# First stage's output projection with the weights stationary: the sum is kept transposed, copied once per batch and turned back

## The chip, the cores and the metric

The kernel runs on one core of one Trainium2 chip. The metric is the device time of one execution in microseconds (us), from the first to the last work of that core. A core has five engines with their own instruction streams: PE (TensorE, matrix products; its weight loads are shown apart as PEld), DVE (VectorE), ACT (ScalarE), POOL (GpSimd) and SP (SyncE, which here only issues DMAs). They wait for one another through semaphores.

## The reference, cut to what matters

A block with 16 batches of 512 tokens and 128 channels. First attention with 16 heads of 64 over a band of 33 keys, then a feed-forward part with attention and a mixture of eight experts. The change touches the last product of the first part and the gate behind it:

```python
h = _layernorm(x, axis=-1) * (1 + ca) + sa
# attention: xn = rms_norm(h); q, k, v; rope; banded softmax; out = attn @ v
out = out.transpose(0, 2, 1, 3).reshape(B, T, H * D)     # (16, 512, 1024)
return out @ w_out.T                                     # (16, 512, 128)
x = x + ga * _L0_attn_ref(h, ...)                        # ga: one gate per batch and channel
```

## The kernel before, in words

The first stage works on items. An item is one batch and one pair of heads (`G = 8` pairs per batch, `NI = 128` items, item i is batch i // 8). Every engine runs the same loop over slots `s`, and each step of an item has a fixed lag behind the slot that starts it: rope of item s, scores of item s-2 (`LS`), softmax of item s-3 (`LE`), transposes of the probabilities of item s-4 (`LT`), the product with the values of item s-5 (`LV`) and the output projection of item s-6 (`LO`). So the order of the work on each engine is written out by hand; only semaphores decide when it starts.

In one slot PE issues, in this order: two rope groups (`matmul` lines 305 to 307, each three products with 512 columns moving, into a PJ bank), the output projection (line 317), 16 small score products (line 331), 16 small products with the values (line 347), in some slots `to_columns` (line 262), then `values` (lines 281 to 283, one group of three into a PJ bank) and eight transposes of probabilities (line 366).

The output projection multiplies the attention output `ot`, which lies with the item's 128 head channels on the partitions and the 512 tokens along the row. Four products per item take 128 tokens each as the stationary operand and the item's `wo` as the moving one; they add up over the batch's eight items in the PSUM bank `ACC` as four blocks of tokens x channels. After the eighth item DVE multiplies `ACC` by the gate in `mod` into `x1` (line 485), POOL adds `xt` (line 569), and SP stores `x1` and loads the input of a later batch (lines 233 and 180). A product with f32 operands appears in the trace as two records.

**The PJ ring.** Two PSUM banks (`PJ`) are used in turn by everything that has to be read back at once: rope groups, `values`, the columns of the next batch's normalized input (`xn`, in slots with s % 8 == 6) and a gate row (`mod`, in slots with s % 8 == 3). The list `plan` holds the uses in order. Before PE writes a use, `bank_of` waits until the use two places earlier in `plan` has been read:

```python
n = pj_use[w]
if n >= 2:
    v = plan[n - 2]
```

What it waits for depends on the kind of that use: for a rope group DVE's second product (line 458), for `values` ACT's copy into `vn` (line 655), and for `xn` the semaphore `s_xl`. The last comes from a chain: `to_columns(b)` on PE, then ACT copies the bank into `xh` (`x_high`, line 596), then DVE writes the rest, bank minus `xh`, into `xl` (`x_low`, line 400). `xh` and `xl` of a batch are what rope and `values` of its items read, from the slot after next on.

ACT works through a slot in the order: two copies into `pT` (line 624), eight exponentials (line 633), the copy into `ot` (line 642), `x_high` in slots with s % 8 == 6, and the copy into `vn` (line 655). DVE's order is: four rope products (lines 457 and 458), eight masked row maxima (line 469), a reciprocal (line 478), line 485 in slots with s % 8 == 5 from s = 13 on, `x_low` in slots with s % 8 == 6. SP issues per slot four DMAs of `sw` (line 207) and two or three of `vw` (lines 217 to 220).

Of the kernel before, what the change touches and what calls it, by code (L numbers as in the profile page):

```python
# [14 lines left out]
P = 128  # L15
NB, T, C = 16, 512, 128
NH, G = 16, 8
NI = NB * G
# [11 lines left out]
def program(nc, a, out, debug=None):  # L30
# [6 lines left out]
    with top:  # L37
        def sbt(ctx, name, shape, dt=F32):
            return ctx.enter_context(nc.sbuf_tensor(name, shape, dt))

        def sem(name):
            return top.enter_context(nc.semaphore(name))
# [3 lines left out]
        ident = sbt(top, "ident", [P, P])  # L46
# [14 lines left out]
        p1 = ExitStack()  # L61
        mod = sbt(p1, "mod", [P, NB, 3 * C])
# [4 lines left out]
        wo = sbt(p1, "wo", [P, G, C])  # L67
# [4 lines left out]
        xn = sbt(p1, "xn", [P, 4, C])  # L72
# [31 lines left out]
        sq = sbt(p1, "sq", [P, C])  # L104
        ot = [sbt(p1, f"ot{n}", [P, T]) for n in range(2)]
        x1 = [sbt(p1, f"x1{n}", [P, 4, C]) for n in range(2)]

        s_x = [sem(f"a_x{n}") for n in range(4)]
        s_ct = sem("a_ct")
# [29 lines left out]
        s_pj = sem("a_pj")  # L139
# [13 lines left out]
        s_ot = sem("a_ot")  # L153
        s_op = sem("a_op")
        s_y = sem("a_y")
        s_x1 = sem("a_xo")
        s_x1d = [sem("a_x1d0"), sem("a_x1d1")]

# [2 lines left out]
        SLOTS = NI + LO + 1  # L161

        plan = [("xn", 0)]
        for s in range(NI):
            plan += [("rope", s, 0), ("rope", s, 1)]
            if s % G == 6 and s // G + 1 < NB:
                plan.append(("xn", s // G + 1))
            if s % G == 3 and s // G + 2 <= NB:
                plan.append(("mod", s // G + 2))
            plan.append(("v", s))  # L170
        pj_use = {w: n for n, w in enumerate(plan)}

        def vd_count(n):
# [2 lines left out]
        with nc.Block() as blk:  # L176
            @blk.sync
            def _(sp):
                def x_in(b):
                    sp.dma_start(xt[b % 4][:, :, :], x_d[:, 4 * b:4 * b + 4, :]).then_inc(s_x[b % 4], 16)  # L180

                x_in(0)
                sp.dma_start(ct[:, :], a["ct"]).then_inc(s_ct, 16)
                for n in range(2):
                    c = slice(384 * n, 384 * n + 384)
                    sp.dma_start(wmod[:, c], a["wmod"][:, c]).then_inc(s_wm[n], 16)
                    if n == 0:
                        sp.dma_start(ident[:, :], a["ident"]).then_inc(s_id, 16)
                for n in range(3):
                    c = slice(1024 * n, 1024 * n + 1024)  # L190
                    sp.dma_start(wf3[:, c], a["wqkv"][:, c]).then_inc(s_wf[n], 16)
                sp.dma_start(cos[:, :], a["cos"]).then_inc(s_cs, 16)
                sp.dma_start(sin[:, :], a["sin"]).then_inc(s_cs, 16)
                sp.dma_start(mf[:, :], a["masks"]).then_inc(s_mf, 16)
                sp.dma_start(wo[:, :, :], a["wo"]).then_inc(s_wo, 16)
                sp.dma_start(b1t[:, :], a["b1"]).then_inc(s_b1, 16)
                for b in range(1, 4):
                    x_in(b)
                sp.wait_ge(s_z, 2)
                for s in range(SLOTS):  # L200
                    if s < NI:
                        sp.wait_ge(s_rope, 2 * s + 2)
                        if s >= 2:
                            sp.wait_ge(s_add, s - 1)
                        for k in range(4):
                            d, m = slice(32 * k, 32 * k + 32), slice(32 * (k ^ 1), 32 * (k ^ 1) + 32)
                            sp.dma_start(sw[s % 2][d, :, :], mm[s % 2][m, 1, :, :]).then_inc(s_sw[s % 2], 16)
                        half, j = divmod(s, 4)
                        v = vw[half % 2]
                        if half >= 2:  # L210
                            sp.wait_ge(s_pv, 4 * (half - 2) + 4)
                        else:
                            sp.wait_ge(s_zi, 1)
                            sp.wait_ge(s_wlo, 3)
                            sp.wait_ge(s_mk, 3)
                        sp.wait_ge(s_ve, s + 1)
                        sp.dma_start(v[32:96, 2 * j, :], vn[j][0:64, :]).then_inc(s_vd[j], 16)
                        sp.dma_start(v[0:96, 2 * j + 1, :], vn[j][32:128, :]).then_inc(s_vd[j], 16)
                        if j < 3:
                            sp.dma_start(v[0:32, 2 * j + 2, :], vn[j][96:128, :]).then_inc(s_vd[j], 16)  # L220
                    if s == NI - 8:
                        for dst, src in ((bc[:, :, :].rearrange("p a b -> p (a b)"), "bc"), (wfa, "fw"), (con, "con"),
                                         (rows, "rows"), (trf, "tri")):
                            sp.dma_start(dst[:, :], a[src]).then_inc(s_l2, 16)
                        sp.dma_start(bkf[:, :], a["blk"][:, 0:P]).then_inc(s_l2, 16)
                        for e in range(2):
                            sp.dma_start(w1s[e][:, :], a["W1"][:, e * DF:(e + 1) * DF]).then_inc(s_ws[e], 16)
                    if s < NE:
                        sp.dma_start(xs_d[NE * STR + s * P:NE * STR + (s + 1) * P, :], zrow[:, :]).then_inc(s_pre, 16)
                    if s >= LO and (s - LO) % G == G - 1:  # L230
                        b = (s - LO) // G
                        sp.wait_ge(s_x1, b + 1)
                        sp.dma_start(x1_d.rearrange("(j p) b c -> b p j c", p=P)[b], x1[b % 2][:, :, :])\
                          .then_inc(s_x1d[b % 2], 16)
                        if b + 4 < NB:
                            x_in(b + 4)
                sp.wait_ge(s_x1d[0], 16 * (NB // 2))
                sp.wait_ge(s_x1d[1], 16 * (NB // 2))
                sp.wait_ge(s_pre, 16 * NE)
                sp.wait_ge(s_b1, 16)  # L240

            @blk.tensor
            def _(pe):
                def bank_of(w):
# [3 lines that stand above are left out]
                        if v[0] == "rope":  # L248
                            pe.wait_ge(s_rope, 2 * v[1] + v[2] + 1)
                        elif v[0] == "v":  # L250
                            pe.wait_ge(s_ve, v[1] + 1)
                        elif v[0] == "mod":
                            pe.wait_ge(s_mev, v[1] + 1)
                        else:
                            pe.wait_ge(s_xl, v[1] + 1)
                    return PJ[n % 2]
# [38 lines left out]
                for s in range(SLOTS):  # L295
# [13 lines left out]
                    if 0 <= i < NI:  # L309
                        b, g = divmod(i, G)  # L310
                        pe.wait_ge(s_ot, i + 1)
                        if i == 0:
                            pe.wait_ge(s_wo, 16)
                        if g == 0 and b:
                            pe.wait_ge(s_y, b)
                        for j in range(4):
                            ins = pe.matmul(ACC[:, j * P:(j + 1) * P], ot[i % 2][:, j * P:(j + 1) * P], wo[:, g, :],  # L317
                                            start=(g == 0 and j == 0), stop=(g == G - 1), skip_group_check=True)
                        ins.then_inc(s_op, 1)
                    i = s - LS  # L320
                    if 0 <= i < NI:
                        if i:
# [28 lines left out]
                    if s < NI:  # L351
                        if s % G == 6 and s // G + 1 < NB:
                            to_columns(s // G + 1)
                        if s % G == 3 and s // G + 2 <= NB:
                            spread(s // G + 2, bank_of(("mod", s // G + 2)))
                        values(s)
                    i = s - LT
                    if 0 <= i < NI:
# [11 lines left out]
            def _(dve):  # L370
# [76 lines left out]
                for s in range(SLOTS):  # L447
# [32 lines left out]
                    if 0 <= i < NI and i % G == G - 1:  # L480
                        b = i // G
                        dve.wait_ge(s_op, i + 1)
                        if b >= 2:
                            dve.wait_ge(s_x1d[b % 2], 16 * (b // 2))
                        dve.tensor_tensor(x1[b % 2][:, :, :], ACC[:, :].rearrange("p (j c) -> p j c", j=4),
                                          mod[:, b:b + 1, 2 * C:].to_broadcast([P, 4, C]), ALU.mult).then_inc(s_y, 1)
                    b, r = s // G + 1, s % G
                    if b < NB:
# [8 lines left out]
            def _(pool):  # L497
# [45 lines left out]
                for s in range(SLOTS):  # L543
# [14 lines left out]
                    if b < NB:  # L558
# [3 lines left out]
                            next(sh)  # L562
                        if r == 4:
                            scale(b)
                    i = s - LO
                    if 0 <= i < NI and i % G == G - 1:
                        b = i // G
                        pool.wait_ge(s_y, b + 1)
# [943 lines left out]
```

## Time and profile before

| | us |
|---|---|
| median of three runs | 1257.46 (1255.93 to 1259.2) |
| the profiled execution | 1253.87 |
| its span, first to last instruction | 1252.1 |
| first stage, from PE's first slot to its last projection | 21.8 to 824.3 |
| PE busy over the span | 1127.8 (90%) |
| ACT, POOL, DVE busy | 931.4, 873.5, 871.3 |
| mean granted clock of TensorE, share of full | 0.952 |

A row of a timeline gives the start, how long it took, the engine, the line, the operation, what it writes and reads, and how many records were merged; in brackets the idle time of the engine before it and what ended that. Records of PE overlap: each lasts until its result is written, while the next may have started; so the time that a group takes from PE is the distance between the starts of two groups, not the sum of the records' lengths.

### The profile page before, as it was taken

Reading aid. Unit: us, or ns where it says so; the run is one execution under the profiler, and the core shown is the slowest. Engines: PE = TensorE matmul, PEld = TensorE weight load, DVE = VectorE, ACT = ScalarE, POOL = GpSimd, SP = SyncE. Lnnn points to the kernel's source line nnn. Section 1 sums busy time; section 2 is a strip of 40 time slices with the busy share of each in tenths; the row PEclk is TensorE's granted clock in tenths of the full one; section 3 lists DMA queues with packets and bytes.
Section 4 is the critical chain, followed back from the end, with each engine's and each line's share of the span. In section 5 each row is a group of like instructions: output and inputs, shape, how many; then the busy total and the mean of one; then the engine's idle time right before and its main releaser. Section 6 shows DMA issues by size and latency. Waiting matters only on the chain. (4 is left out here: it accounts for less than half of the span.)

```text
span 1252.1 us, 50490 instructions
## 1 busy us (share of the span) xinstructions
PE 1127.8 (90%) x18097; PEld 957.1 (76%) x18097; DVE 871.3 (70%) x4013; ACT 931.4 (74%) x3429; POOL 873.5 (70%) x705
## 2 busy tenths in 40 slices
PE   4899999999999999999999999948889883599991
PEld 2688888888888888888888888836678773588881
DVE  6777777777786777877777866636678864177663
ACT  3789888889889898898898898837767652366660
POOL 3787776777777777767777776645466777178885
PEclk9999999999999999999999999979989985699996
DMA  5766666666666666666666667524143224575110
GB/s 175 200 175 164 160 158 161 150 170 158 153 170 157 158 164 147 166 160 151 168 165 148 161 157 189 139 87 153 50 133 95 73 79 154 159 199 153 56 34 24
DMA packets 108262, 177.55 MB, mean 142 GB/s; under 512 B 19294, under 2 KB 61537, under 8 KB 107888
## 3 DMA queue, kind: packets, MB, share of 16 engines
q1 hardware_dynamic: 100176, 155.14, 48.3%
q0 software_dynamic: 6400, 16.82, 3.8%
q8 instruction: 148, 2.42, 0.8%
q10 hardware_dynamic: 1440, 2.36, 0.7%
q14 instruction: 98, 0.80, 0.2%
HBM read 31.86 MB, written 24.68 MB: 45 GB/s over the span
## 5 line engine op out<-in xcount | busy, mean ns | idle before, releaser
L549 POOL TENSOR_TENSOR qk<-mm,sw 128x1024 f32<-128x1024 f32 x128 | 303.9, 2374 | 120.5 <-DMA sw<-mm 120.5
L633 ACT ACTIVATE pr<-sm,mn 128x96 f32<-128x96 f32 x1024 | 368.5, 370 | 0.2 <-DVE mn L469 0.2
L457 DVE TENSOR_TENSOR mm<-bank,cos 128x512 f32<-128x512 f32 x256 | 175.3, 685 | 175.6 <-PE bank L307 165.5
L555 POOL TENSOR_TENSOR pr<-pr,ri 128x768 f32<-128x768 f32 x128 | 188.2, 1470 | 77.2 <-DVE ri L478 75.2
L633 ACT ACTIVATION_READ_ACCUMULATOR pr<-sm,mn 128x1 f32 x1024 | 201.9, 197 | 0.0
L469 DVE CUSTOM_DVE_ANT_0 sm<-bank,msk 128x96 f32<-128x96 f32 x1024 | 192.0, 252 | 5.3 <-PE bank L331 5.3
L458 DVE TENSOR_TENSOR mm<-bank,sin 128x512 f32<-128x512 f32 x256 | 174.0, 680 | 0.0
L347 PE MATMUL bank<-pT,vw 96*64 96x64 f32 x4096 | 147.5, 225 | 0.0
L317 PEld LDWEIGHTS bank<-wo,ot 128*128 128x128 f32 x1024 | 133.4, 191 | 14.2 <-ACT ot L642 3.2
L347 PEld LDWEIGHTS bank<-pT,vw 96*64 96x64 f32 x4096 | 129.8, 138 | 15.2
L624 ACT ACTIVATE pT<-bank 96x512 f32<-96x512 f32 x256 | 137.3, 588 | 0.0
L317 PE MATMUL bank<-wo,ot 128*128 128x128 f32 x1024 | 135.1, 275 | 2.3 <-ACT ot L642 2.3
L366 PE MATMUL bank<-ident,pr 128*96 128x128 f32 x1024 | 132.7, 273 | 0.0
L366 PEld LDWEIGHTS bank<-ident,pr 128*96 128x96 f32 x1024 | 115.7, 126 | 18.7
L1225 ACT ACTIVATE fv<-bank,b1t 128x128 f32<-128x128 f32 x288 | 82.2, 368 | 54.8 <-PE bank L1088 53.6
L642 ACT ACTIVATE ot<-bank 128x512 f32<-128x512 f32 x128 | 76.2, 595 | 62.0 <-PE bank L347 62.0
L305 PE MATMUL bank<-xh,wh 128*128 128x512 f32 x256 | 113.8, 444 | 4.6 <-DVE xl L400 1.4
L331 PE MATMUL bank<-qk 64*64 64x96 f32 x4096 | 114.1, 249 | 2.9 <-POOL qk L549 2.9
L655 ACT ACTIVATE vn<-bank 128x512 f32<-128x512 f32 x128 | 76.2, 595 | 42.7 <-PE bank L283 42.7
L331 PEld LDWEIGHTS bank<-qk 64*64 64x64 f32 x4096 | 89.9, 133 | 19.7 <-issue 2.9
L306 PE MATMUL bank<-xl,wh 128*128 128x512 f32 x256 | 101.9, 398 | 0.0
L307 PE MATMUL bank<-xh,wl 128*128 128x512 f32 x256 | 101.6, 397 | 0.0
(195 smaller groups left out, 2333.0 us busy)
## 6 DMA issues: line engine op xcount, KB each, us to landing
sw<-mm SPq DMA_DIRECT2D x512, 128.0 KB, 2.3
vw<-vn SPq DMA_DIRECT2D x128, 192.0 KB, 2.5
vw<-vn SPq DMA_DIRECT2D x128, 128.0 KB, 2.3
rr<-sorted_scratch SPq DMA_DIRECT2D x72, 192.5 KB, 3.0
vw<-vn SPq DMA_DIRECT2D x96, 64.0 KB, 2.2
xt<-in_x SPq DMA_DIRECT2D x16, 256.0 KB, 4.3
x_scratch<-x SPq DMA_DIRECT2D x16, 256.0 KB, 2.7
rr<-x_scratch SPq DMA_DIRECT2D x16, 256.0 KB, 3.0
```

The source lines that it names most:

```text
L305: pe.matmul(dst[:, :], wh[:, o:o + P], xh[b % 2][:, :], start=True, stop=False)
L317: ins = pe.matmul(ACC[:, j * P:(j + 1) * P], ot[i % 2][:, j * P:(j + 1) * P], wo[:, g, :], start=(g == 0 and j == 0), stop=(g == G - 1), s ...
L331: ins = pe.matmul(SC[h][64 * e:64 * e + 64, p * WK:(p + 1) * WK], t[r, 0, 32 + 64 * w:96 + 64 * w], t[r, 1, 64 * w:64 * w + WK], start=Tru ...
L347: ins = pe.matmul(OB[64 * h:64 * h + 64, 64 * w:64 * w + 64], vw[half % 2][:, w, c:c + 64], pT[i % 2][:, h, 64 * w:64 * w + 64], start=Tru ...
L366: ins = pe.transpose(TR[h][0:WK, p * P:(p + 1) * P], pr[i % 2][:, h, p, :], ident[:, :])
L457: dve.tensor_tensor(mm[s % 2][:, 0, j, :], PJ[u % 2][:, :], cos[:, :], ALU.mult)
L458: dve.tensor_tensor(mm[s % 2][:, 1, j, :], PJ[u % 2][:, :], sin[:, :], ALU.mult)\
L469: ins = dve.tensor_tensor_reduce(ms_[i % 2][:, h, p, :], SC[h][:, p * WK:(p + 1) * WK], msk[:, min(p, 1), :], 1.0, 3.0e38, ALU.add, ALU.mi ...
L549: pool.tensor_tensor(qk[i % 2][:, :, 32:], mm[i % 2][:, 0, :, :], sw[i % 2][:, :, :], ALU.add)\
L555: pool.tensor_tensor(t, t, ri[i % 2][:, :].unsqueeze(2).to_broadcast([P, 8, WK]), ALU.mult)\
L624: act.activation(pT[i % 2][:, h, :], TR[h][0:WK, :], ACT.Copy).then_inc(s_te, 1)
L633: ins = act.activation(pr[i % 2][:, h, p, :], ms_[i % 2][:, h, p, :], ACT.Exp, scale=-1.0, bias=mn[i % 2][:, h, p:p + 1], accum_out=sums[i ...
```

## The change

The output projection swaps its operands. `wo` of the item is stationary and all 512 tokens of `ot` move, in one product per item; `ACC` then holds the sum transposed, channels x tokens. After the batch's eighth item DVE copies it into a new tile `yt`. One slot later PE turns `yt` back by four transposes into a PJ bank, and DVE multiplies that bank by the gate. So `plan` has a new use, `yt`, before `values` in every slot with s = 14, 22, ..., 134, and POOL's addition and SP's store and load move one slot later. PE's wait before the first projection of a batch is for the copy (`s_yt`) and no longer for the gate product (`s_y`).

```diff
-        for s in range(NI):
-            plan += [("rope", s, 0), ("rope", s, 1)]
...
+        for s in range(SLOTS):
+            if s < NI:
+                plan += [("rope", s, 0), ("rope", s, 1)]
+                if s % G == 6 and s // G + 1 < NB:
+                    plan.append(("xn", s // G + 1))
+                if s % G == 3 and s // G + 2 <= NB:
+                    plan.append(("mod", s // G + 2))
+            if s > LO and (s - LO - 1) % G == G - 1:
+                plan.append(("yt", (s - LO - 1) // G))
+            if s < NI:
+                plan.append(("v", s))
...
+                        elif v[0] == "yt":
+                            pe.wait_ge(s_y, v[1] + 1)
...
-                            pe.wait_ge(s_y, b)
-                        for j in range(4):
-                            ins = pe.matmul(ACC[:, j * P:(j + 1) * P], ot[i % 2][:, j * P:(j + 1) * P], wo[:, g, :],
-                                            start=(g == 0 and j == 0), stop=(g == G - 1), skip_group_check=True)
-                        ins.then_inc(s_op, 1)
+                            pe.wait_ge(s_yt, b)
+                        pe.matmul(ACC[:, :], wo[:, g, :], ot[i % 2][:, :], start=(g == 0), stop=(g == G - 1))\
+                            .then_inc(s_op, 1)
...
+                    i = s - LO - 1
+                    if 0 <= i < NI and i % G == G - 1:
+                        b = i // G
+                        dst = bank_of(("yt", b))
+                        pe.wait_ge(s_yt, b + 1)
+                        for j in range(4):
+                            ins = pe.transpose(dst[:, j * P:(j + 1) * P], yt[:, j * P:(j + 1) * P], ident[:, :])
+                        ins.then_inc(s_pj, 1)
+                    if s < NI:
                         values(s)
...
                         dve.wait_ge(s_op, i + 1)
+                        if b:
+                            dve.wait_ge(s_pj, pj_use[("yt", b - 1)] + 1)
+                        dve.tensor_copy(yt[:, :], ACC[:, :]).then_inc(s_yt, 1)
+                    i = s - LO - 1
+                    if 0 <= i < NI and i % G == G - 1:
+                        b = i // G
+                        u = pj_use[("yt", b)]
+                        dve.wait_ge(s_pj, u + 1)
                         if b >= 2:
                             dve.wait_ge(s_x1d[b % 2], 16 * (b // 2))
-                        dve.tensor_tensor(x1[b % 2][:, :, :], ACC[:, :].rearrange("p (j c) -> p j c", j=4),
+                        dve.tensor_tensor(x1[b % 2][:, :, :], PJ[u % 2][:, :].rearrange("p (j c) -> p j c", j=4),
                                           mod[:, b:b + 1, 2 * C:].to_broadcast([P, 4, C]), ALU.mult).then_inc(s_y, 1)
```

PE's rows in slot 14 before, from the last product with the values to the next slot's first rope group (`a_xl` is the semaphore `s_xl`, `a_rope` is `s_rope`):

```order
245 L262 MATMUL bank<-ident,xn 128x128 [waits a_xn,a_rope]
246 L262 MATMUL bank<-ident,xn 128x128 x3
247 L281 MATMUL bank<-wh,xh 128x512 [waits a_rope]
248 L282 MATMUL bank<-wl,xh 128x512
249 L283 MATMUL bank<-wh,xl 128x512
250 L366 MATMUL bank<-ident,pr 96x128 [waits a_te,a_nm]
251 L366 MATMUL bank<-ident,pr 96x128 x3
252 L366 MATMUL bank<-ident,pr 96x128 [waits a_te]
253 L366 MATMUL bank<-ident,pr 96x128 x3
254 L305 MATMUL bank<-xh,wh 128x512 [waits a_xl]
```

The same place of the changed kernel, whose lines 270, 289 and 313 are lines 262, 281 and 305 of before, and whose line 381 is line 366:

```order
236 L270 MATMUL bank<-ident,xn 128x128 [waits a_xn,a_rope]
237 L270 MATMUL bank<-ident,xn 128x128 x3
238 L368 MATMUL bank<-ident,yt 128x128 [waits a_yt,a_rope]
239 L368 MATMUL bank<-ident,yt 128x128 x3
240 L289 MATMUL bank<-wh,xh 128x512 [waits a_xl]
241 L290 MATMUL bank<-wl,xh 128x512
242 L291 MATMUL bank<-wh,xl 128x512
243 L381 MATMUL bank<-ident,pr 96x128 [waits a_te,a_nm]
244 L381 MATMUL bank<-ident,pr 96x128 x3
245 L381 MATMUL bank<-ident,pr 96x128 [waits a_te]
246 L381 MATMUL bank<-ident,pr 96x128 x3
247 L313 MATMUL bank<-xh,wh 128x512 [waits a_y]
```

The four transposes of `yt` stand between `xn` and `values`; the wait for `s_xl` has moved from the next slot's rope group up to `values`, and the rope group waits for `s_y`.

DVE's rows in the changed kernel at the end of the maxima of the same slot (`a_pj` counts PE's finished uses of the ring; `x` is `x1`); before, the reciprocal was followed by `xl` at once:

```order
323 L493 RECIPROCAL ri<-sums 128x8 [waits a_nm,a_exp]
324 L508 TENSOR_TENSOR x<-bank,mod 128x512 [waits a_pj]
325 L415 TENSOR_TENSOR xl<-bank,xh 128x512 [waits a_xh]
326 L472 TENSOR_TENSOR mm<-bank,cos 128x512 [waits a_sw1,a_add,a_pj]
```

The gate product has come from the slot before to a place ahead of `x_low`.

## Rows read from the trace of the kernel before

**Rows 1.** The page: busy us and shares; the projection's group, mean ns behind the bar

```profile
PE 1127.8 (90%) x18097; PEld 957.1 (76%) x18097; DVE 871.3 (70%) x4013; ACT 931.4 (74%) x3429; POOL 873.5 (70%) x705
...
L317 PE MATMUL bank<-wo,ot 128*128 128x128 f32 x1024 | 135.1, 275 | 2.3 <-ACT ot L642 2.3
```

**Rows 2.** Windows: busy time of each engine in one batch (eight slots)

```profile
361.52:410.81 49.29, 49.16 (x722) 42.20 (x719) 37.08 (x184) 43.38 (x176) 36.40 (x24) 1.00 0.64 160
```

**Rows 3.** Waits, 65 to 755 us: total, times, longest

```profile
PEld bank L305 <- DVE xl L400: 5.4, 14, 0.4
```

**Rows 4.** Timeline of PE, parts of two undisturbed slots

```profile
780.67 0.39 PE L306 MATMUL bank<-xl,wh 128*128 128x512 f32 x1
780.89 0.39 PE L307 MATMUL bank<-xh,wl 128*128 128x512 f32 x1
...
781.83 1.05 PE L317 MATMUL bank<-wo,ot 128*128 128x128 f32 x8
782.81 0.89 PE L331 MATMUL bank<-qk 64*64 64x96 f32 x32
...
787.79 1.05 PE L317 MATMUL bank<-wo,ot 128*128 128x128 f32 x8
```

**Rows 5.** Timeline of PEld in the second stage, f32 with 512 moving

```profile
855.74 0.30 PEld L1000 LDWEIGHTS bank<-hT,wfa 128*128 128x128 f32 x2
856.27 0.19 PEld L1000 LDWEIGHTS bank<-hT,wfa 128*128 128x128 f32 x1 [0.24 <-issue]
856.70 0.19 PEld L1000 LDWEIGHTS bank<-hT,wfa 128*128 128x128 f32 x1 [0.24 <-issue]
```

**Rows 6.** Timeline of PE in a slot with xn

```profile
402.47 0.66 PE L262 MATMUL bank<-ident,xn 128*128 128x128 f32 x4
402.88 0.48 PE L281 MATMUL bank<-wh,xh 128*128 128x512 f32 x1
...
404.84 0.50 PE L305 MATMUL bank<-xh,wh 128*128 128x512 f32 x1
```

**Rows 7.** Timeline of ACT in the same slot and the next

```profile
403.00 0.59 ACT L642 ACTIVATE ot<-bank 128x512 f32<-128x512 f32 x1
403.47 0.59 ACT L596 ACTIVATE xh<-bank 128x512 fp32r<-128x512 f32 x1
...
409.33 0.60 ACT L642 ACTIVATE ot<-bank 128x512 f32<-128x512 f32 x1 [0.96 <-PE bank L347]
```

**Rows 8.** Timeline of DVE, the slot before and the slot with xn

```profile
397.11 0.64 DVE L485 TENSOR_TENSOR x<-bank,mod 128x512 f32<-128x512 f32 x1
...
404.09 0.69 DVE L400 TENSOR_TENSOR xl<-bank,xh 128x512 fp32r<-128x512 f32 x1 [0.76 <-ACT xh L596]
```

**Rows 9.** Timeline of the first stage's end, PE and DVE

```profile
823.13 1.16 PE L317 MATMUL bank<-wo,ot 128*128 128x128 f32 x8 [0.69 <-ACT ot L642]
...
824.33 0.69 DVE L485 TENSOR_TENSOR x<-bank,mod 128x512 f32<-128x512 f32 x1 [7.46 <-PE bank L317]
...
829.20 0.45 PE L967 MATMUL bank<-ident,bc 128*128 128x128 f32 x1 [4.91 <-PEq L176]
```

**Rows 10.** Timeline of SP's DMA issues in the slot with xn and the next

```profile
405.98 0.81 SPq L217 DMA_DIRECT2D vw<-vn  x1
...
407.47 0.60 SPq L220 DMA_DIRECT2D vw<-vn  x1
408.35 2.42 SPq L207 DMA_DIRECT2D sw<-mm  x4
```

**Rows 11.** Timeline of POOL, behind them

```profile
408.11 2.38 POOL L549 TENSOR_TENSOR qk<-mm,sw 128x1024 f32<-128x1024 f32 x1 [3.23 <-DMA sw<-mm]
```

**Rows 12.** Windows: columns as in rows 2, with the granted clock as a share

```profile
30.00:35.00 5.00, 2.52 (x39) 1.75 (x38) 2.28 (x6) 0.06 (x1) 3.62 (x2) 1.00 0.86 224
35.50:38.90 3.40, 3.26 (x11) 1.97 (x14) 1.96 (x18) 2.92 (x14) 2.67 (x2) 0.51 0.80 225
...
815.00:824.00 9.00, 7.26 (x107) 6.50 (x104) 0.20 (x1) 5.34 (x17) 1.47 (x1) 1.00 0.02 4
```

More of the change, by code:

```diff
@@ L106, in program @@
         x1 = [sbt(p1, f"x1{n}", [P, 4, C]) for n in range(2)]
+        yt = sbt(p1, "yt", [P, T])
         s_x = [sem(f"a_x{n}") for n in range(4)]
@@ L155, in program @@
         s_y = sem("a_y")
+        s_yt = sem("a_yt")
         s_x1 = sem("a_xo")
@@ L163, in program @@
         plan = [("xn", 0)]
-        for s in range(NI):
-            plan += [("rope", s, 0), ("rope", s, 1)]
[L166 to L170, printed above, removed]
+        for s in range(SLOTS):
[9 more added lines that the diff above has]
+                plan.append(("v", s))
         pj_use = {w: n for n, w in enumerate(plan)}
@@ L229, in _ @@
                         sp.dma_start(xs_d[NE * STR + s * P:NE * STR + (s + 1) * P, :], zrow[:, :]).then_inc(s_pre, 16)
-                    if s >= LO and (s - LO) % G == G - 1:
-                        b = (s - LO) // G
+                    if s > LO and (s - LO - 1) % G == G - 1:
+                        b = (s - LO - 1) // G
                         sp.wait_ge(s_x1, b + 1)
@@ L564, in _ @@
                             scale(b)
-                    i = s - LO
+                    i = s - LO - 1
                     if 0 <= i < NI and i % G == G - 1:
```

## The prediction

> **What bounds the kernel now.** I began with the page's busy shares [rows 1]: PE leads with 90% of the whole span, but that mixes two stages. The windows over one batch of the first stage [rows 2] separate them: in 49.29 us PE is busy for 49.16, at the full clock, while ACT has 43.38 and DVE 37.08. The waits of the stage say where the little rest is: PE waits in only one place that counts, 14 times before line 305, 5.4 us in all [rows 3]. So in the first stage every microsecond that PE gains or loses is the kernel's. A slot takes PE 5.96 us from projection to projection [rows 4], and 128 of them make up the stage.
>
> The one wait of PE deserves the close look, because the change passes through it. It stands in the slots with `xn`. There [rows 6] PE turns `xn` at 402.47, goes on with `values` at 402.88 and the transposes of probabilities, and arrives at the next rope group before its bank is free; that group starts at 404.84. What it waited for is a chain on two other engines. ACT comes out of its exponentials at 403.0, copies `ot`, and then writes `xh` from 403.47 to 404.06 [rows 7]. DVE has waited 0.76 us for that and writes `xl` from 404.09 to 404.78 [rows 8]. Today PE covers most of this chain with `values` and line 366.
>
> **The projection itself.** It removes 8 records per item and adds 2. Today the 8 take 1.05 us to the last one's end; with 0.27 us for the last record itself (the mean in [rows 1]) they follow one another every (1.05 - 0.27) / 7 = 0.111 us, so 8 use 0.89 us. From the first to the start of line 331 it is 0.98 us [rows 4], so that 0.09 us belongs to the change of tile shape ahead of line 331; I leave it. The nearest rows for the new form are line 1000's, the same f32 type and 128x128 weights with 512 columns moving. Their weight loads, one per record, follow every 0.43 us at full clock [rows 5]. Two make 0.86 us. So four times the columns cost four times the time, and an item gains 0.03 us: 128 x 0.03 = 4 us. The weight loads that disappear (six per item) were hidden behind the products and return nothing. Bounds: at best the long second record also hides the 0.09, and an item gains 0.12 us, 15 us in all; at worst the first record pays what line 1000's first pays (0.53 against 0.43, from the load at 855.74 to that at 856.27, after another tile shape), and an item loses 0.07, 9 us in all. I take 0.03, because the product ahead of the projection (line 307) has the full tile shape and is long enough to cover a load of 0.19.
>
> Against this stands a rule. The Trainium skill, "TensorE: Matmul & The Clock Gate", section "Back-to-back issue gap", gives for sustained streams of load and product about 81 ns each with 128 columns and 131 ns with 512; by it, four products of 128 would become one of 512 at 131 / 324 = 0.40 of their time, 0.98 would become 0.40 us, and 128 items would gain some 75 us. No row here shows such a gap for f32: [rows 5] have 0.43 us per record of 512, four times the 0.111 of [rows 4].
>
> **The four transposes.** 4 records of f32 per batch at the same 0.11 us: 0.44 us of PE. In slot 126, where there is no `xn`, that is all: the gate product is then covered by `values` and line 366.
>
> **The ring.** This is the large term. `yt` takes a place in `plan` between `xn` and `values`. `values` used to wait for the slot's second rope group, long read; two places back it now finds `xn`, and that means `s_xl`: PE stands before `values`, without the 1.6 us of work that used to cover the chain. Also, DVE has the gate product ahead of `x_low`. Worked out for the slot of [rows 6]:
> - line 262 ends at 402.47 + 0.66 = 403.13; the transposes of `yt` follow and end 0.44 later, 403.57.
> - the gate product, 0.64 us [rows 8], runs from 403.61 to 404.25. `xh` is ready at 404.06 [rows 7], so it is no longer what is late.
> - `x_low` can start a little before that end (DVE's products follow about 0.6 apart), at 404.20, and ends 0.69 later, 404.89.
> - PE begins `values` 0.06 after it, as line 305 does today (404.78 to 404.84): 404.95 where it was 402.88.
> - from `values` to the rope group is 404.84 - 402.88 - 0.38 of waiting = 1.58 us, and 0.03 more for a start from idle: 406.56 against 404.84.
>
> The batch loses 1.7 us on PE, the 0.44 of the transposes included. It happens where `xn` and `yt` meet: slots 14, 22, ..., 118, 14 times: 23.8 us. Bounds: 1.6 if DVE's order cost nothing and only ACT's copy counted; 1.9 if DVE starts the gate product later than I put it.
>
> What is late next: `vn` is copied when `values` is done, about 405.9 to 406.5 instead of 403.95, so ACT starts the next slot about 2.1 us late while PE is 1.7 late. ACT has 0.96 us of waiting before its next `ot` [rows 7], which covers 0.4. SP waits for `vn` before its three issues; they begin at 406.5 rather than 405.98 and take 2.1 [rows 10], and the store and load that the change moves into this slot add some 1.2: 409.9. The next `sw` is due at 408.35 + 1.7 = 410.05. That just fits, and behind it POOL idles 3.23 us for `sw` [rows 11]. POOL's addition, which moves in there, fits too. I cost all three at nothing.
>
> **The end of the stage.** After the last projection comes the chain PE, DVE, POOL, store, and then the second stage's first PE row at 829.20 [rows 9], covered by nothing. It gets a copy (0.69), the transposes from idle (0.66 + 0.1) and two hand-overs (0.09): 1.5 us. The copies of the other batches take the place of a gate product of the same size on DVE [rows 8], which had been finished at 397.75, long before it was wanted; nothing.
>
> **The sum.** 14 x 1.7 + 0.44 + 1.5 - 4 = +21.7 us on the profiled execution's 1253.87, which gives 1275.6. The median of the runs shown is 3.6 us above that execution, so the median should be 1257.46 + 21.7 = 1279. Differences under 0.3%, 3.8 us, are about what a measurement of this kernel cannot tell from none.
>
> **Rivals.**
> - *The stall costs more* (11 in 100). Either the clock falls in it, or the SP queue, which has only 0.15 us to spare, makes the next slot late. For the clock: after a stretch in which PE was busy for 2.52 of 5 us it ran at 0.51, which is the 1.2 GHz level, for 3.4 us [rows 12]; in the stage's last slots, 7.26 of 9 busy, it stayed at 2.4 GHz. The new slot is idle for about 1.5 us at one time and dense on both sides, nearer to the second. If it fell for one such stretch per batch, PE would lose half of 3.26 us each time: 14 x 1.6 = 23 us more, 1302; in half of the batches 1290.
> - *The wait is covered anyway* (4 in 100): `x_low` would have to end by 403.3, when PE is through with `yt`. The rows give 404.78 even without the gate product in front. Then the sum is 15 x 0.44 + 1.5 - 4 = +4, 1261, and within 0.3% if the 0.09 of line 331 is hidden in part.
> - *The projection gets much cheaper* (5 in 100; this one ends faster). If f32 with 512 moving ran at the pace of lines 306 to 307, 0.23 us from start to start [rows 4], an item would take 0.46 + 0.09 = 0.55 instead of 0.98: 55 us gained against 26 lost, 1228. It decides from 0.2 us per item on (26 / 128). For it: one load instead of four per pass, and the rule above. Against it: line 1000's records do not run at that pace in this same kernel [rows 5].
>
> **The numbers.** My case has 80 in 100. Its own range comes from the bounds: item gain 15 gives 1268, item loss 9 gives 1292, and 1.6 to 1.9 per batch moves it by -1 to +3. The range 1268 to 1292 leaves out the two rivals below it, 9 in 100, and most of the one above. Faster by over 0.3%: 0.05. Within 0.3%: 0.04. Slower: 0.91.
>
> **What the profile after would show.** If I am right: two records per item some 0.43 apart and about 0.95 us from the projection to the scores; slots without a new use at 5.92 to 5.93 instead of 5.96; in every eighth slot PE idle for some 1.5 us before `values`, released by `x_low`, and no wait left before the rope group; that slot 1.7 longer; the first stage's end 1.5 later than its last projection explains; the clock at full. I am wrong if the pair of records is under 0.4 us (then faster), or if the wait stands but the next slot is also longer (then the first rival).

## The result and the profile after

The changed kernel takes 1277.58 us (median, 1275.91 to 1282.43) where the kernel before took 1257.35 in the same session: 1.0173 times the time, with a 95% interval from 1.0141 to 1.0205. It is 20.2 us slower; the forecast was 21.7 slower, 1279. Ratios compare fast executions only: one of the kernel with the copies swapped and the loads spread, 1422.61 us at a granted clock of 0.73, counts in its median but not in its ratio.

The profiled execution is the slowest of the four, 1282.43 us. So I read it in two parts, cut where PE starts the second stage, at 829.20 before [rows 9] and at 851.17 now. The first stage has become 22.0 us longer. The windows over the second stage, which the change does not touch, first of the kernel before and then of the changed one (length, busy time and records of PE, PEld, DVE, ACT and POOL, granted clock, busy share of the DMA engines, GB/s):

```profile
829.20:1252.10 422.90, 329.46 (x6603) 279.39 (x6603) 270.21 (x1078) 231.70 (x639) 281.32 (x326) 0.86 0.35 107
```

```profile
851.20:1280.60 429.40, 336.90 (x6603) 286.03 (x6603) 271.09 (x1078) 232.19 (x639) 282.67 (x326) 0.83 0.35 105
```

It has the same 6603 records of PE and took 6.5 us more in this execution, at a mean clock of 0.83 instead of 0.86. Over all the kernels profiled here it takes 421 to 429 us, with no relation to what was edited. The first stage is the place to compare.

The page of the changed kernel, busy shares and the projection's group:

```profile
PE 1138.8 (89%) x17393; PEld 886.3 (69%) x17393; DVE 882.8 (69%) x4029; ACT 933.9 (73%) x3429; POOL 874.6 (68%) x705
...
L324 PE MATMUL bank<-ot,wo 128*128 128x512 f32 x256 | 131.0, 593 | 2.4 <-ACT ot L665 2.4
```

1024 records have become 256, each about twice as long. PE is busy 11 us longer than before [rows 1] although it has fewer instructions; 7.4 of the 11 lie in the second stage (336.90 against 329.46). One batch (columns as in [rows 2]):

```profile
370.04:420.73 50.69, 49.31 (x677) 37.28 (x675) 37.52 (x184) 43.55 (x175) 36.73 (x24) 1.00 0.62 154
```

A batch takes 50.69 us instead of 49.29, and PE is no longer busy in all of it: 1.38 us are idle. The waits from 65 to 770 us say where:

```profile
ACT vn L678 <- PE bank L291: 51.3, 98, 1.8
...
PEld bank L289 <- DVE xl L415: 22.6, 14, 1.6
PE bank L289 <- DVE xl L415: 19.3, 14, 1.4
...
DVE x L508 <- PE bank L368: 3.1, 14, 0.2
```

The wait of [rows 3] before the rope group is gone. In its place PE stands 14 times before `values` (line 289), 19.3 us in all, until DVE has written `xl`. And ACT, which waited up to 0.4 us for `values`, now waits up to 1.8. An undisturbed slot on PE, beside [rows 4]:

```profile
802.11 1.02 PE L324 MATMUL bank<-ot,wo 128*128 128x512 f32 x2
803.06 0.89 PE L337 MATMUL bank<-qk 64*64 64x96 f32 x32
...
808.03 1.02 PE L324 MATMUL bank<-ot,wo 128*128 128x512 f32 x2
```

The projection takes 0.95 us to the start of the scores instead of 0.98, and the slot 5.92 instead of 5.96. The slot with `xn` and `yt`, PE, beside [rows 6]:

```profile
410.85 0.66 PE L270 MATMUL bank<-ident,xn 128*128 128x128 f32 x4
411.35 0.60 PE L368 MATMUL bank<-ident,yt 128*128 128x128 f32 x4
413.33 0.50 PE L289 MATMUL bank<-wh,xh 128*128 128x512 f32 x1 [1.38 <-DVE xl L415]
...
414.92 0.47 PE L313 MATMUL bank<-xh,wh 128*128 128x512 f32 x1
```

The same stretch on DVE, beside [rows 8]:

```profile
411.55 0.20 DVE L493 RECIPROCAL ri<-sums 128x8 f32<-128x8 f32 x1
411.98 0.69 DVE L508 TENSOR_TENSOR x<-bank,mod 128x512 f32<-128x512 f32 x1 [0.23 <-PE bank L368]
412.59 0.68 DVE L415 TENSOR_TENSOR xl<-bank,xh 128x512 fp32r<-128x512 f32 x1
```

And on ACT, beside [rows 7]:

```profile
411.89 0.59 ACT L619 ACTIVATE xh<-bank 128x512 fp32r<-128x512 f32 x1
414.32 0.60 ACT L678 ACTIVATE vn<-bank 128x512 f32<-128x512 f32 x1 [1.84 <-PE bank L291]
...
419.36 0.60 ACT L665 ACTIVATE ot<-bank 128x512 f32<-128x512 f32 x1 [0.60 <-PE bank L353]
```

From line 270 to `values` it is 2.48 us where it was 0.41; from there to the rope group 1.59. The transposes of `yt` end at 411.95, DVE takes the bank at 411.98, starts `xl` 0.61 later, and PE goes on 0.06 after its end. What SP does behind it:

```profile
414.99 0.50 SPq L223 DMA_DIRECT2D vw<-vn  x1
...
417.45 0.53 SPq L186 DMA_DIRECT2D xt<-in_x  x1
418.40 3.29 SPq L213 DMA_DIRECT2D sw<-mm  x4
```

SP is through at 417.98 and is wanted at 418.40. The end of the stage, beside [rows 9]:

```profile
843.63 1.12 PE L324 MATMUL bank<-ot,wo 128*128 128x512 f32 x2 [0.69 <-ACT ot L665]
844.79 0.69 DVE L500 COPY yt<-bank 128x512 f32<-128x512 f32 x1 [7.40 <-PE bank L324]
...
845.63 0.63 PE L368 MATMUL bank<-ident,yt 128*128 128x128 f32 x4 [0.88 <-DVE yt L500]
846.29 0.69 DVE L508 TENSOR_TENSOR x<-bank,mod 128x512 f32<-128x512 f32 x1 [0.81 <-PE bank L368]
...
851.17 0.45 PE L990 MATMUL bank<-ident,bc 128*128 128x128 f32 x1 [4.91 <-PEq L182]
```

From the start of the last projection to the second stage it is 7.54 us, against 6.07 before: 1.5 more.

### The profile page after: what moved, and what is told of

Read it like the earlier page. It is cut to its first block and busy times, and to the rows that moved or that the text cites. A ratio compares the mean times of both kernels' runs of the same rounds, so it can differ in the third digit from the quotient of the medians.

```text
span 1280.6 us, 49129 instructions
## 1 busy us (share of the span) xinstructions
PE 1138.8 (89%) x17393; PEld 886.3 (69%) x17393; DVE 882.8 (69%) x4029; ACT 933.9 (73%) x3429; POOL 874.6 (68%) x705
## 5 line engine op out<-in xcount | busy, mean ns | idle before, releaser
L324 PE MATMUL bank<-ot,wo 128*128 128x512 f32 x256 | 131.0, 593 | 2.4 <-ACT ot L665 2.4
L974 POOL DMA_INDIRECT out<-h,rr x72 | 80.5, 1118 | 20.1 <-issue 19.8
```

Source lines behind the costliest of these rows:

```text
L324: pe.matmul(ACC[:, :], wo[:, g, :], ot[i % 2][:, :], start=(g == 0), stop=(g == G - 1))\
```

## The experiments

The theory is the ring's: the loss is PE's wait for `xl` ahead of `values`, which the new use in `plan` brings there. The rivals are that the added work costs wherever it stands, that DVE's order does it, and for the product alone that its price is another. "Second stage at" is the start of PE's first row of the second stage; "batch" is the distance from one rope group on PE to the one eight slots later.

| kernel | batch, us | second stage at | time, us |
|---|---|---|---|
| before | 49.29 | 829.20 | 1257.35 |
| changed | 50.69 | 851.17 | 1277.58 |
| turn one slot later | 49.48 | 834.56 | 1261.6, ratio 1.0036 (1.0012 to 1.0061) |
| wait alone | 50.87, three of 52.4 | 855.63; again 855.19 | 1280.0; again 1283.84, 1.021 (1.0168 to 1.0252) |
| product alone | 49.07 | 830.75; again 828.53 | 1257.86; again 1256.98, 0.9987 (0.996 to 1.0014) |
| x_low first | 50.63 | 850.63 | 1278.46 |
| yt ahead of xn | 49.76 | 836.95 | 1261.41 |
| ACT's copies swapped | 49.00 | 825.24 | 1253.62, 0.9978 (0.996 to 0.9995) |
| turn later and copies swapped | 49.13 | 827.91 | 1258.48, 1.0016 (0.9996 to 1.0036) |
| copies swapped, loads spread | 49.00 | 823.95 | 1250.1, 0.9939 (0.9915 to 0.9963) |
| product alone, loads spread | 49.07 | 824.93 | 1252.15, 0.9951 (0.9932 to 0.997) |

Below the first two rows a time without a ratio is that of a single execution. Since the second stage moves by several microseconds from one execution to the next, the batch and the second stage's start decide.

**The turn one slot later.** Three engines, SP and the plan use `s - LO - 2` where the change has `s - LO - 1`, and there is one slot more:

```diff
-            if s > LO and (s - LO - 1) % G == G - 1:
-                plan.append(("yt", (s - LO - 1) // G))
+            if s > LO + 1 and (s - LO - 2) % G == G - 1:
+                plan.append(("yt", (s - LO - 2) // G))
```

> The changed kernel, with the turn of yt, the gate product, POOL's addition and the store one slot later (slots with s % 8 == 7), where no xn is in the ring, so that values waits for a rope group again. Ring theory (the loss is PE's wait for xl before values): the batch of eight slots returns from 50.69 us to 49.30 + 0.44 (transposes) - 0.24 (eight cheaper projections) = 49.50, and the second stage's first PE row, at 829.2 before and 851.2 after the change, comes at about 834.5; the time is some 5 us over that of before. Rival (the copy, the turn and the gate product cost their 1.4 us per batch wherever they stand): it stays near 851.

The batch is 49.48, the second stage starts at 834.56. Of the 1.40 us per batch that the change costs, 1.21 are gone though all of its work is still done. The rival falls. `yt` in a slot without `xn` costs its transposes and no more. In its waits, 65 to 780 us, PE's wait for `xl` stands before the rope group again (line 313) and is short as in [rows 3], and none for `xl` stands before `values`:

```profile
PEld bank L313 <- DVE xl L415: 6.2, 14, 0.4
```

**The wait alone**, in the kernel before:

```diff
                             spread(s // G + 2, bank_of(("mod", s // G + 2)))
+                        if s % G == 6 and s > G and s // G + 1 < NB:
+                            pe.wait_ge(s_xl, s // G + 2)
                         values(s)
```

> The kernel before with one line more: in the 14 slots where the change has its wait, PE waits for xl before values. No transpose, no copy, old projection. Ring theory: values starts at about 404.84 instead of 402.88 and covers nothing any more, 1.6 us per batch, 14 x 1.6 = 22.5, second stage at about 851.7. Rival (it is the added work, not the wait): 829.

> The same kernel as in the run with the wait alone, once more and timed. There the clock fell to its lower level in 3 of 14 waiting slots and cost 1.6 us each time. If that depends on where the waits fall in time, other batches than the first time, and another number of them, are 52.4 us long, and the rest 50.87; the time is 24 to 30 us over that of before, more than the changed kernel's. If it is bound to fixed batches, the same three are long.

One wait, with no work added, makes the batch 50.87: 1.6 us, as costed, and more than the whole change costs per batch, since there the cheaper projections give 0.24 back and the transposes lie inside the wait. The second stage starts 4 us later than the theory said, and the granted clock is why. Timeline of PE in the seventh of its 14 waiting slots:

```profile
413.84 0.65 PE L262 MATMUL bank<-ident,xn 128*128 128x128 f32 x4
416.21 0.74 PE L281 MATMUL bank<-wh,xh 128*128 128x512 f32 x1 [1.72 <-DVE xl L402]
...
419.17 0.73 PE L305 MATMUL bank<-xh,wh 128*128 128x512 f32 x1
```

Windows over that stretch:

```profile
413.00:416.30 3.30, 1.58 (x37) 1.28 (x33) 2.30 (x18) 2.43 (x11) 2.61 (x2) 1.00 0.90 252
416.30:419.70 3.40, 3.40 (x12) 2.86 (x13) 0.00 (x0) 1.34 (x3) 1.21 (x1) 0.50 0.32 80
419.70:423.00 3.30, 3.30 (x56) 2.80 (x56) 2.60 (x5) 3.30 (x17) 1.18 (x1) 1.00 0.43 119
```

After a wait of 1.72 us, with PE busy for 1.58 of 3.3 us, the clock goes to 0.50, the 1.2 GHz level, while PE is working without a gap, and returns 3.4 us later. From line 281 to line 305 it takes 2.96 us instead of 1.6. Three batches of 14 are longer by 1.5 to 1.6 for this, 4.8 us together. All 14 waits are 1.71 or 1.72 us long, and behind 11 of them the clock stayed at 1.00. The clock fell in slots 22, 62 and 94 in this execution and in slots 22, 54 and 94 in the second: the number repeated and two of the three slots, so neither of the two cases of the second expectation came out. In the changed kernel the wait is 1.38 us and the clock stayed at 1.00 behind all 14.

**The product alone**, in the kernel before; the sum stays transposed and is multiplied as it stands, so the kernel leaves the turn back out and its output is another:

```diff
-                        for j in range(4):
-                            ins = pe.matmul(ACC[:, j * P:(j + 1) * P], ot[i % 2][:, j * P:(j + 1) * P], wo[:, g, :],
-                                            start=(g == 0 and j == 0), stop=(g == G - 1), skip_group_check=True)
-                        ins.then_inc(s_op, 1)
+                        pe.matmul(ACC[:, :], wo[:, g, :], ot[i % 2][:, :], start=(g == 0), stop=(g == G - 1))\
+                            .then_inc(s_op, 1)
```

> The kernel before with the projection's operands swapped and nothing else: the transposed sum goes through the gate product as if it were not transposed, so the turn back is left out and the output is another. My price for the product: 0.03 us per item, slots of 5.93 instead of 5.96, second stage at 829.2 - 4 = 825.2. The rule of the rival (0.40 of the time): 75 us less, 754. If the first record of the pair pays for its load: 838.

> The same kernel as in the run with the product alone (the turn back is left out, the output is another), once more and timed, because one slot near the first stage's end took 11.6 us there instead of 6 to 7. If that was the DMA traffic of that execution and not the product, the batch is 49.07 us again, the slot is under 8 us, the second stage starts at 825 to 827, and the time is 3 to 4 us under that of before. If the new product does it, the slot is long again and the time is that of before or more.

> The kernel with the product alone (the turn back is left out, the output is another), with the same spread of the loads. There the slot took 11.6 and 10.4 us in two executions. If it is the burst that meets a more unlucky place in SP's order, the slot is 5.93 and the second stage starts at 829.2 - 4 = 825.2 at the latest, and this is the price of the product free of the burst. If the new product itself makes the slot long, it stays over 10.

The batch is 49.07, 0.22 less, 0.028 per item: my price. But the second stage did not come at 825.2. In slot 120 SP issues eight loads for the second stage at once, and slot 123 took 11.6 us and, in the second execution, 10.4; I had expected under 8 there. Timeline of POOL and of PE in the first one:

```profile
773.31 2.34 POOL L547 TENSOR_TENSOR qk<-mm,sw 128x1024 f32<-128x1024 f32 x1 [8.08 <-DMA sw<-mm]
...
775.79 1.56 PE L329 MATMUL bank<-qk 64*64 64x96 f32 x32 [2.79 <-POOL qk L547]
```

POOL waits 8.1 us for `sw`, and PE 2.8 us for POOL. The clock falls too: it is at 0.50 from 775.16 on, still in that wait, for 6.8 us; in the second execution, where PE waits 2.85 us, it falls 1.6 us after the wait, for 3.4 us. In the second, 2.85 of waiting leave 1.6 of the 4.5 us that the slot is too long, which is what a stretch of 3.4 us at that clock cost in the run with the wait alone. With the loads issued one per slot in slots 104 to 111 the slot is 5.93, and the second stage starts at 824.93. So the product does not make it long without the burst of loads. With the burst, the same slot takes 6.59 us before the change, 7.15 in the changed kernel and 5.96 to 7.67 in the others; PE waits at most 1.7 us there, and the clock stays at 1.00. Why `sw` is later with the product alone (POOL waits 8.1 us for it, 5.9 before) stays open: SP issues the same DMAs in the same order in both kernels.

**x_low ahead of the gate product**, in the changed kernel: the four lines of `centre` and `x_low` stand before the block of the gate product on DVE.

```diff
+                    b, r = s // G + 1, s % G
+                    if b < NB:
+                        if r == 1:
+                            centre(b)
+                        if r == 6:
+                            x_low(b)
                     i = s - LO - 1
                     if 0 <= i < NI and i % G == G - 1:
```

> The changed kernel with DVE's x_low ahead of the gate product in the slots where both stand. If ACT's copy into xh is what is late next, only 0.1 us per batch returns, 1.5 us in all, second stage at about 850. Rival (the gate product ahead of x_low is the loss): 0.6 us per batch, second stage at about 842.

The batch is 50.63, 0.06 less, and the second stage at 850.63. DVE's order is worth under a microsecond; the rival said 9. ACT's copy is next: in its waits DVE stands 14 times, up to 0.8 us, before `xl` until ACT has written `xh`.

**yt ahead of xn**, in the changed kernel, in `plan` and in PE's order:

```diff
             if s < NI:
                 plan += [("rope", s, 0), ("rope", s, 1)]
+            if s > LO and (s - LO - 1) % G == G - 1:
+                plan.append(("yt", (s - LO - 1) // G))
+            if s < NI:
                 if s % G == 6 and s // G + 1 < NB:
                     plan.append(("xn", s // G + 1))
```

> The changed kernel with the two uses in the other order: yt ahead of xn, in the ring and on PE. Two places before values now stands yt, so PE waits for the gate product and no longer for xl, and the next rope group waits for xl as before the change. Ring theory: values starts some 0.9 us earlier than in the changed kernel (the gate product can run from 0.1 us after the reciprocal), the batch is 49.8 us instead of 50.69, the second stage starts at about 838. Rival (the added work costs wherever it stands in the slot): it stays near 851.

49.76 and 836.95. Nothing but the place of one entry has changed and 14 us come back: exactly the use two places before `values` decides. Its waits name the other one now:

```profile
PEld bank L289 <- DVE x L508: 9.5, 14, 0.7
...
PE bank L289 <- DVE x L508: 6.1, 14, 0.4
```

**ACT's two copies swapped**, alone and with the turn one slot later. In slots with s % 8 == 6 `x_high` stands ahead of the copy into `ot`:

```diff
+                    b, r = s // G + 1, s % G
+                    if r == 6 and b < NB:
+                        x_high(b)
                     i = s - LV
                     if 0 <= i < NI:
                         act.wait_ge(s_pv, i + 1)
```

> The kernel before with ACT's two copies swapped in the slots with xn: first xh, then ot. It moves the chain that PE waits for 0.47 us forward: xl ends at about 404.4, when PE is just through with line 366. The wait of 0.38 us before line 305 goes, 15 x 0.36 = 5.4 us less, second stage at about 823.8, time about 1252. Rival (ot half a microsecond later delays the next projection or the next product with the values): no change or slower.

> The turn one slot later and ACT's copies swapped. If both work as costed they add up: second stage at about 829, the time of before. The projection's gain of 0.24 us per batch does not pay for the transposes' 0.44, so it stays behind the kernel before with the copies swapped alone by some 5 us.

Alone it takes 0.29 us off the batch (0.36 expected) and PE's wait before the rope group is gone from the waits. Together they make 49.13: 49.48 less 0.35. The sum is level with before within its interval; the cheaper product does not pay for its transposes.

**And the loads spread:**

```diff
-                    if s == NI - 8:
-                        for dst, src in ((bc[:, :, :].rearrange("p a b -> p (a b)"), "bc"), (wfa, "fw"), (con, "con"),
-                                         (rows, "rows"), (trf, "tri")):
+                    if NI - 24 <= s < NI - 16:
+                        k = s - NI + 24
...
```

> The kernel before with ACT's two copies swapped, and SP's eight loads for the second stage issued one per slot in slots 104 to 111 instead of all in slot 120. With the copies alone, one slot behind the burst took 6.91 us instead of 5.96. If the burst makes sw late there, that slot returns to 5.96 and the second stage starts at about 824.3 instead of 825.2; the time is 5 us under that of before. Rival (the loads only move their delay into eight other slots): the second stage starts at 825 or later.

The slot behind the burst is 5.96, no other has grown, and the second stage starts at 823.95. At 0.9939 this kernel is faster than the kernel before and than the changed one, with the projection in its old form.

## Why the prediction was right

- *PE bounds the first stage.* Right: 14 times the change of the batch, the lower clock where it fell, slot 123 and the 1.5 at the end give the second stage's start in every kernel here to within 1.4 us.
- *The projection gains 0.03 us per item.* Measured 0.028 alone, 0.95 against 0.98 in the profile. The records of [rows 5] follow every 0.43 us here too. The rival at a pace of 0.23 is out. So is, for f32 products with hidden weight loads, the rule of the Trainium skill, "TensorE: Matmul & The Clock Gate", "Back-to-back issue gap", by which 75 us would have been gained; the measurement decides.
- *The four transposes cost 0.44.* With the turn one slot later the batch is 49.48 against 49.07 with the product alone: 0.41. In the slot of the wait they cost nothing, since they lie in it; I had counted that in.
- *The ring costs 1.7 per batch.* Slot with `xn`: 8.39 instead of 6.74, 1.65, or 1.68 without the projection's gain. The place was the one named; the wait alone, and its removal by moving `yt` in two ways, show that it is the cause.
- *What is late next costs nothing.* ACT's wait before `ot` shrank from 0.96 to 0.60 (0.56 by my count), SP had 0.4 us to spare instead of the 0.15 that I gave it.
- *The end costs 1.5.* It cost 1.5.
- *The stall costs more* (11 in 100) did not come about in this kernel, but the run with the wait alone came close to it: behind 1.72 us of waiting, 0.3 more than here, the clock fell in 3 of 14 slots at 1.6 us each, the price that I had written for it.

The sum for the first stage was 21.7, and 22.0 came: 14 x 1.40 = 19.6 for the full batches (23.8 - 14 x 0.24 = 20.4 in the prediction), 1.5 at the end, and 0.6 in slot 123, behind the burst of loads, which the sum did not have. The rest, 0.3, lies in the other slots from 120 to 127 and the start. So the mechanism and its price were right, but that the two totals lie 0.3 apart is partly luck: the batches came 0.8 under their term, and 0.9 that the sum did not have made up for it. In the medians it was 20.2; the second stage moves by several microseconds from one execution to the next, and the difference of 1.5 is within the interval.

## What to carry to other kernels

When a new use enters a ring of two buffers, look at who now stands two places before whom: the cost here was not the new work (0.4 us) but a reader at the end of a chain over two other engines, ACT and DVE, which PE now awaited with nothing left to cover it (1.6 us). Put such a use where its neighbours are read early. An f32 record took 0.11 us from start to start with 128 moving columns and 0.43 with 512, so four products of 128 columns and one of 512 cost nearly the same here, where the weight loads are hidden. And if the bound engine waits at all, even 0.4 us once in 49, look at the order on the engines behind that wait: one swap on ACT gave more than the new product.

## What was not expected of the hardware

The granted clock fell after a wait of 1.72 us in the middle of dense work, in 3 of 14 slots in each of two executions, and stayed at 1.00 after 14 waits of 1.38 us. It also fell in or behind the wait of 2.8 us in slot 123 of both executions of the product alone. Eight loads issued back to back in slot 120 made `sw` late: slot 123 took from 5.96 to 11.6 us over the kernels here, the lower clock included, and 5.93 to 5.96 once they were spread.
